# First layer's routing in three groups of batches instead of two, its first group placed ahead of the last batch; GpSimd stores the experts' results and SyncE only loads weights

## What is computed

```python
x = x + _L0_xattn_ref(_layernorm(x), ctx_768, ...)     # 16 heads of 16
x = x + _L0_ffn_ref(_layernorm(x), ...)
# _L0_ffn_ref, x of 800 rows by 256, 8 experts, hidden 1024:
gate_logits = jnp.einsum('btd,de->bte', x, Wg) + bg
gate_scores = jax.nn.softmax(gate_logits, axis=-1)
top1_idx = jnp.argmax(gate_scores, axis=-1)            # one expert for each row
h = jax.nn.silu(jnp.einsum('btd,edh->bteh', x, W1) + b1)
o = jnp.einsum('bteh,ehd->bted', h, W2) + b2
y = jnp.sum(o * top1_mask[..., None], axis=2) * top1_weight
...
x = x + _L1_xattn_ref(...)                              # second layer
x = x + _L1_ffn_ref(...)
```

## Time and profile before

| | |
|---|---|
| time, 3 runs | 704.38, 705.5, 707.92 us; median 705.5 |
| the profiled execution's own time | 702.82 us |
| its span, first to last instruction | 701.1 us |
| busy PE, PEld, DVE, ACT, POOL | 90%, 71%, 55%, 57%, 36% |
| mean granted clock of TensorE | 0.955 of full |
| first layer's routing and wait for rows | about 200 to 225 us |
| its experts | 225 to 314 us |

### The profile page before, as it was taken

One profiled execution on the slowest core, in us unless ns is written; L12 is line 12 of the kernel. 1 busy time (PEld: TensorE's weight loads), 2 busy tenths in 40 slices (PEclk: granted clock), 3 DMA queues, 4 the chain that ended last, 5 costly groups with the idle time before them and its releaser, 6 DMA issues.

```text
span 701.1 us, 15177 instructions
## 1 busy us (share of the span) xinstructions
PE 629.5 (90%) x4728; PEld 500.6 (71%) x4729; DVE 384.0 (55%) x1176; ACT 399.7 (57%) x961; POOL 249.3 (36%) x339
## 2 busy tenths in 40 slices
PE   2999789999986999989999989999997899999992
PEld 1777456666665888986788756666765798999992
DVE  5222467777734001108988754545775667666661
ACT  1444689998842334235576697767351455555550
POOL 6012355557647000002100000000032688888880
PEclk9999799999975999999999999999997999999995
DMA  6116910004431488403110010000022877677774
GB/s 153 32 47 203 328 48 2 2 1 152 134 115 40 147 274 279 148 33 91 35 49 8 0 52 1 1 2 1 1 94 71 222 194 189 179 188 195 191 186 119
DMA packets 76331, 73.76 MB, mean 105 GB/s; under 512 B 10966, under 2 KB 69876, under 8 KB 76152
## 3 DMA queue, kind: packets, MB, share of 16 engines
q1 hardware_dynamic: 69200, 64.45, 30.2%
q0 software_dynamic: 4240, 6.50, 5.1%
q10 hardware_dynamic: 2840, 2.17, 1.1%
HBM read 57.78 MB, written 15.31 MB: 104 GB/s over the span
## 4 chain that ended last, share of the span: by engine, by line
PE 60%; ACT 10%; DVE 9%; issue 7%; DMA 6%; POOL 4%; SPq 2%; DVEq 1%; POOLq 0%; ACTq 0%
PE psum L1254 4%; PE psum L1241 4%; ACT probs L793 4%; PE psum L630 3%; PE psum L644 3%; PE psum L1743 3%; PE psum L1765 3%; PE psum L1752 3%; DMA v_all<-in_L_ffn_W_dram 3%; PE psum L723 3%; PE psum L713 2%; PE psum L1791 2%; PE psum L2345 2%; PE psum L2347 2%; PE psum L2346 2%
## 5 line engine op out<-in xcount | busy, mean ns | idle before, releaser
L793 ACT ACTIVATE probs<-probs,negmax 100x361 f32<-100x361 f32 x128 | 68.9, 587 | 10.5 <-POOL probs L858 10.4
L873 DVE TENSOR_SCALAR_CACHE_REDUCE probs<-psum 100x361 f32<-100x361 f32 x128 | 60.6, 530 | 17.9 <-PE psum L713 17.9
L723 PEld LDWEIGHTS psum<-ident,probs 100*128 100x128 f32 (+1 forms) x384 | 39.4, 156 | 27.0 <-issue 18.7
L723 PE MATMUL psum<-ident,probs 100*128 100x100 f32 (+1 forms) x384 | 47.6, 262 | 11.1 <-ACT probsT L801 5.2
L858 POOL TENSOR_SCALAR probs<-probs 100x722 f32<-100x722 f32 x64 | 50.4, 788 | 5.1
L1284 ACT ACTIVATE kT_all<-psum,kT_all 128x128 f32<-128x128 f32 x88 | 25.1, 368 | 47.3 <-PE psum L1241 47.3
L2235 POOL TENSOR_TENSOR xT_low<-kT_all,xT_high 128x1600 fp32r<-128x1600 f32 x1 | 3.6, 3561 | 129.4 <-ACT xT_high L2206 129.4
L1241 PE MATMUL psum<-kT_all,v_all 128*128 128x128 f32 x352 | 43.4, 283 | 6.0 <-DMA v_all<-in_L_ffn_W_dram 2.9
L1241 PEld LDWEIGHTS psum<-kT_all,v_all 128*128 128x128 f32 x352 | 42.0, 198 | 8.9 <-issue 5.3
L2345 PE MATMUL psum<-xT_high,we_high 128*128 128x400 f32 x128 | 45.3, 354 | 2.9 <-issue 2.9
L2347 PE MATMUL psum<-xT_high,we_low 128*128 128x400 f32 x128 | 44.8, 350 | 0.0
(11 more groups left out here) (442 smaller groups left out, 1716.3 us busy)
## 6 DMA issues: line engine op xcount, KB each, us to landing
v_all<-in_L_ffn_W_dram SPq DMA_DIRECT2D x16, 1024.0 KB, 7.7
xs_dram<-zeros SPq DMA_DIRECT2D x1, 7424.0 KB, 23.5
kT_all<-coefT_dram SPq DMA_DIRECT2D x18, 400.0 KB
v_all<-in_L_ffn_Wg_dram SPq DMA_DIRECT2D x36, 128.0 KB
v_all<-in_L_ffn_Wu_dram SPq DMA_DIRECT2D x36, 128.0 KB
v_all<-in_L_ffn_Wd_dram SPq DMA_DIRECT2D x36, 128.0 KB
ctx_nat<-in_ctx_dram SPq DMA_DIRECT2D x16, 192.0 KB
rank_rows<-rank_dram SPq DMA_DIRECT2D x18, 100.0 KB, 3.5
```

What stands on the lines that cost most here:

```text
L723: last = nc.tensor.transpose(pT_ps[0:rows[t], t, hh * NQ:(hh + 1) * NQ], probs[:, n % NPB, hh, t * P:t * P + rows[t]], ident[0:NQ, 0:NQ])
L793: last = nc.scalar.activation(row, row, ACT.Exp, bias=negmax[:, n % NPB, hh:hh + 1])
L873: last = nc.vector.tensor_scalar(probs[:, n % NPB, hh, 0:NKV], psum[0:NQ, n % 2 * 2 + hh, 0:NKV], -CLAMP, None, ALU.max, ALU.max, accum_ou ...
```

## The change

It does eight things.

1. `sets` becomes three groups: batches 0 to 3, 4 to 6, and 7. The functions that had SET and two groups in them take each group's own size. Ranks of a later group start from `gate_prior_sums`, the sum of `choice` over all batches before, which DVE makes once a group (`gate_prior`), where a matmul for each batch did it before.
2. `begin_ranks`, `rank` and `gate_place` of group 0 move into the first attention, ahead of the last batch's transposes back and its addition.
3. The layer norm of batches 4 to 6 moves from POOL to DVE (`normalise0`); ACT loads the table of the square root with one extra instruction before it copies `take_tail`, and takes the roots after it.
4. `totals_ps` becomes one matmul over 64 columns in place of eight over 8; a reduction on DVE replaces the copy. The transposition of `b1` moves behind it.
5. On ACT the first block's rows are loaded before `act_top_weight`; DVE takes the sums after the first block's rows. PE's six products of zeros start when all groups are placed and the blocks are known, not after the second of three counts.
6. At the start of the first attention PE gets 12 products of zeros.
7. POOL stores `ys_rows` (`pool_experts`) and clears the spare rows of `sum_dram`; SP's loop over blocks goes.
8. SP loads W1 of expert e + 2 once the hidden layer of expert e's last block is done, and W2 once its output is; the signal `expert_begun` goes.

```diff
-    sets = [slice(k * SET, (k + 1) * SET) for k in range(2)]
+    sets = [slice(0, SET), slice(SET, B - 1), slice(B - 1, B)]
...
         for m in range(2):
             scores(m)
+            products_of_zeros0(o_zeros, 4 if m == 0 else 2)
         for m in range(M0):
             transposes(2 * m)
+            if m == 0:
+                products_of_zeros0(o_zeros, 2)
...
         finish_transpose(B - 1)
+        gate_transposes(pe, SET, B - 1 - SET)
+        begin_ranks(pe, 0)
+        rank(pe, 0)
         finish_transpose_back(B - 1)
-        gate_transposes(pe, SET, B - 1 - SET)
         finish_project(B - 1)
...
         finish_take(B - 1)
-        finish_takeT(B - 1)
         take_gate(act, 4, 2)
         take_gate(act, 6, 1)
+        finish_takeT(B - 1)
...
         dve_late_roots0(dve)
+        for k in range(SET, B - 1):
+            normalise0(k)
         gate_weigh(dve, 0)
+        gate_pick(dve, 0)
         normalise(B - 1)
-        gate_pick(dve, 0)
+        gate_prior(dve, 0)
+        gate_place(dve, 0)
         add(B - 1)
...
+    def gate_prior(dve, k):
+        dve.wait_ge(choice_ready, k + 1)
+        nc.vector.tensor_reduce(gate_prior_sums[k], choice[:, 0:sets[k].stop, :].rearrange("q b e -> q e b"), AX.X, ALU.add
+                                ).then_inc(prior_ready, 1)
...
         gate_weigh(dve, 1)
         gate_pick(dve, 1)
+        gate_prior(dve, 1)
         gate_place(dve, 1)
+        gate_weigh(dve, 2)
+        gate_pick(dve, 2)
+        gate_place(dve, 2)
...
-        step(dve, nc.vector.tensor_copy(tokens, totals_ps))
+        step(dve, nc.vector.tensor_reduce(tokens, totals_ps.rearrange("p (b e) -> p e b", b=B), AX.X, ALU.add))
...
+    def begin_ranks(pe, k):
+        nc.tensor.matmul(ranks_ps[k], ones_row[0:1, 0:NQ], region[:, 0:gate_shape(k)[1] * E0], start=True, stop=False)
+        if k > 0:
+            pe.wait_ge(prior_ready, k)
+            nc.tensor.matmul(ranks_ps[k], ones_sq[:, 0:NQ], gate_prior_sums[k - 1].unsqueeze(1).broadcast_to(gate_shape(k)),
+                             start=False, stop=False)
...
     def pe_gate(pe):
         gate_products(pe, SET, B - 1 - SET)
+        begin_ranks(pe, 1)
         gate_transposes(pe, B - 1, 1)
+        rank(pe, 1)
         gate_products(pe, B - 1, 1)
+        begin_ranks(pe, 2)
+        rank(pe, 2)
+        nc.tensor.matmul(totals_ps, ones_sq[:, :], choice[:, :, :], start=True, stop=True).then_inc(ranks_ready, 1)
...
+    def pool_experts(pool):
+        def block(n, at, i, p, first):
+            pool.wait_ge(ys_ready, n + 2)
+            pool.dma_start(ys_dram[bass.ds(at * P, P), :], ys_rows).then_inc(ys_stored, 16)
+
+        pool.dma_start(sum_dram[B * NQ:B * NQ + P, :], zeros[:, :]).then_inc(ys_stored, 16)
+        each_block(pool, block)
...
     def sp_experts(sp):
+        sp.wait_ge(slots_ready, 4)
+        for e in range(E0 - 2):
+            end = sp.value_load(per_expert_i[0:1, 2, e:e + 1], min_val=1, max_val=NBLK)
+            sp.wait_ge(hidden_in_psum, 2 * end)
+            sp_load_w1(sp, e + 2, e % 2)
+            sp.wait_ge(ys_in_psum, end)
+            sp_load_w2(sp, e + 2, e % 2)
...
-        pe.wait_ge(slots_ready, 2)
-        products_of_zeros0(6)
+        pe.wait_ge(slots_ready, 4)
+        products_of_zeros0(late_zeros, 6)
...
         load_rows(0)
+        act_top_weight(act)
         act.wait_ge(rows_used, 1)
...
         def _(pe):
             pe_project0(pe)
+            pe.wait_ge(consts_ready, N_CONSTS + N_MOE_CONSTS)
+            products_of_zeros0(o_zeros, 4)
```

140 lines of the change are left out of this document (62 added, 78 removed).

## The result

The changed kernel took 688.21, 689.04, 689.11 and 691.36 us, median 689.08; the kernel before, run beside it four times, had a median of 706.71 (704.38 to 709.43). The ratio is 0.9754, with an interval of 0.9709 to 0.9799: 2.5% faster. The profiled execution took 689.11 us with a span of 687.5, against 702.82 and 701.1, so 13.6 us of span are to be found. The medians lie 17.6 us apart: the profiled execution before was 3.9 us faster than the median of the four, while the one after stands at its median, and the profiles cannot say where those 4 us lie.

The account below looks back on a forecast made before the run. It saw time lost where PE stands or runs slowly, PE holding 60% of the last-ending chain. Terms -2.2 - 7.3 - 1.3 - 4.7 + 1.1 = -14.4 us gave 688.4 profiled, 691.1 as median; range 684 to 699.

Parts of the forecast that it names:

- Start of the attention: First attention: zeros on PE hold the clock for scores, transposes and values; -2.2 us, bounds +1.0 and -3.9.
- the bound of -3.9: Start of the attention: most the zeros could gain, from 7.9 us of half-speed PE work in a 10.4 us window.
- To the counts: Last batch and routing: norms on DVE, three groups and one totals matmul bring the counts 5.2 us earlier; bounds -3 and -6.
- To the load of rows: Counts to load of rows: fast cast, top weight out of the way, last scatter then late; -7.3 us in all, counts included.
- rival 1: Routing: POOL becomes the bound, load of rows gains 4 not 7.3 us, block 0 nothing of the clock; 695.7 us, chance 0.14.
- Block 0: First expert block: later zeros cut PE's idle time from 4.1 to 1.4 us, raising the clock; -1.3 us, bounds 0 and -1.7.
- Weights: Blocks 1 to 6: weights asked for two experts ahead, waits go and blocks last 7.26 us; -4.7 us, bounds -1.5 and -4.9.
- Rival 2: Experts: weights stay late because transfers set the pace at 268 GB/s; the term is -1.5, the time 694.3 us, chance 0.12.
- Rival 3: Start of the attention and block 0: the zeros do nothing at both places; 694.6 us, chance 0.10.
- Last store: End of the experts: DVE, SP and POOL wait for POOL's last store, which is not hidden; +1.1 us, between 0 and +1.3.
- Rival 4: Experts: POOL's stores hold DVE's bias addition, which waits for the previous block's store; slower, 712 us, chance 0.04.
- rival 5: Behind the experts: gain given back through gathers and keys starting late after POOL's loop; +10 us or more, 702 us, chance 0.05.

Follow-up runs that it names:

- e1: The changed kernel without its 12 products of zeros at the start of the first attention; median 703.34 us, ten runs from 688.43 to 710.29.
- e4: The changed kernel with the totals as eight matmuls of 8 columns and a copy, as before; 694.08 us in one run.
- e7: The changed kernel with one extra silu on ACT ahead of block 0, so its table loads early; median 690.38 us, ratio 0.9768 to the kernel before.
- e9: The kernel before with only the stores on POOL and SP loading weights two experts ahead, W1 and W2 apart; median 701.79 us, ratio 0.9932.
- after: The changed kernel itself, with all eight parts of the change, against the kernel before; median 689.08 us, ratio 0.9754.
- e2: The changed kernel with the top weight's work back ahead of the first load of rows on ACT and first rows on DVE; 694.01 us, one run.
- e3: The changed kernel with SP loading weights one expert ahead, asked for once PE begins an expert, stores still on POOL; median 691.56 us, ratio 0.9761.
- e8: The changed kernel with the early silu table, three zero products instead of four before first scores and five instead of six before block 0; median 691.16 us.
- e11: The changed kernel without the attention's startup zeros, but with 12 products of the same shape at the start of PE's program; median 688.51 us, ratio 0.9775.
- e12: The changed kernel, its zeros kept, with 12 more products at the start of PE's program; median 687.34 us, ratio 0.9765 to the kernel before.
- e6: The changed kernel without its six products of zeros ahead of block 0's rows; median 697.64 us, ratio 0.9913 to the kernel before.
- e10: The changed kernel with experts 0 and 1 written out ahead of PE's loop, so expert 0's block register loads before the transposes; median 691.54 us, ratio 0.9809.
- e5: The changed kernel with the experts' results stored from ACT's queue instead of POOL's; median 699.87 us, ratio 0.9907 to the kernel before.

## Why the prediction was right, and where not

**Start of the attention.** -2.2 predicted, -1.70 measured, by the mechanism named: no window near 0.5, scores at 0.87 us. From first scores to last values it is 2.0 us (120.9 to 118.9), less the 0.3 by which the first scores start later; `e1`, with the change's other edits in the attention but without the zeros, took 120.4, so up to 0.5 of the 2.0 may be theirs. The zeros were costed 0.3 us too short at each score (1.92 us for four). Taken away they cost 1.04 us in one kernel and 4.60 in another: the bound of -3.9 counted only the window up to 85 us, and the clock can stay low for longer.

**To the counts.** -5.2 predicted, 206.03 against 212.88 less the 1.70, so -5.15. Its parts: from the last values to the last batch's x -0.78 instead of -0.3, so -4.37 instead of -4.9 for the rest. The one product for the totals took 0.67 (0.5 taken), and `e4` gives 2.82 for it by itself. The projection was put at 1.0 us and took 1.39: the clock fell in the middle of it, and in other kernels with the same routing it took from 1.11 (`e1`) to 2.03 (`e7`). What is left beside the totals, the layer norms on DVE and the three groups, was read from rows only; no kernel undoes them one by one.

**To the load of rows.** -7.3 predicted, -7.40 measured. Cast at 0.16, load behind the last scatter, as forecast, and `e4` shows the scatter to be the bound by 1.4 us. The last scatter started at 207.91; from the predicted 209.3 less the start's 1.7, it was 0.3 us late. The Trainium skill's rule that GpSimd and VectorE share an interface, with contention for a VectorE instruction in a two-port mode or with two SBUF inputs ("GPSIMD Engine Reference", "1. Specifications"), agrees with the slow subtraction of both kernels in which they met, before and `e9` (2.28 us each), which has two inputs. The cast has one (1.65 and 2.27 us), and whether it ran in a two-port mode no trace shows. In after they miss each other by 0.08 us; the prediction had the subtraction behind the cast, near 211, but not that the moved transposition of `b1` gives it its place there, and put only 0.14 on rival 1.

**Block 0.** -1.3 predicted, -0.86 measured: the step mis-sized. The hidden layer fell to 3.83 as said, the zeros outlasted the rows by 0.7 us, but "block 0 should take 7.3" left out ACT's table load of 1.28 us. It had been hidden under the slow hidden layer before (226.57 in a layer that ended at 230.5) and was not hidden under the fast one. It lasted 8.20; `e7`, without the table load in the way, 7.39. The registers of PE's sequencer, part of the idle time ahead of block 0, were not seen either. That the clock held was in part luck: `e2` and `e3` have the same zeros, and `e8` five products for six, and their hidden layers took 5.46, 5.46 and 5.32 us.

**Weights.** -4.7 predicted, -4.11 measured; distances of 7.58 once, then 7.32 to 7.40, and not 7.26, but no wait for weights. `e3` separates what the prediction gave as three causes together: SP asked late because it stored first, and two experts ahead are not needed. Rival 2 is refuted: 273 GB/s were enough. Rival 3 is too, at the start by `e11` against `e12` (4.60 us); at block 0 `e6` shows the slow hidden layer, but its stop hides what the late zeros are worth in time.

**Last store.** +1.1 predicted, +0.72 measured. Issue to landing took 2.0 us, between the 1.7 of SP's store and the 3.0 of a gather; the latter was the wrong neighbour. The rest lies ahead of the issue, where POOL takes 0.68 us from DVE's addition. The Trainium skill's 0.4 us of difference in the first byte ("DMA: Bandwidth & Descriptors", "Specifications") is near the 0.3 measured from issue to landing, and the sum by it (+0.4) nearer in that part and too low in all. Rival 4, POOL's stores holding DVE, did not come: their median landing in the experts is 4.3 us after issue, and no DVE row there waits for a store.

**Behind the experts.** -0.23, nothing predicted, so rival 5 did not come; the same code varies by 5 us from kernel to kernel, so the 0.23 tells nothing. Sum: -14.4 predicted, -13.6 measured between the two profiled spans. As a median the prediction was 691.1, of which 2.7 us were the distance of the median before from its profiled execution; after had no such distance, so 689.08 lies below it although the span fell by less than forecast. That these two errors partly cancel is luck.

## What to carry to other kernels

When one link of a chain is shortened, work out which other one is late next and by how much: of the 2.82 us that the totals gave, half stayed under the scatters, and a table load that a slow clock had hidden came out when the clock rose. A queue that both asks for loads and waits for stores asks late; move the waiting one to an engine whose other work is not waited for (POOL here, not ACT). To test what filler products on TensorE are worth, move them instead of taking them out, since taking out can change more than the clock.

## What was not expected of the hardware

Both kernels with fewer instructions in PE's list than after by a whole group of products (`e1` and `e6`, twelve and six products) had stops of PE of 2.06 to 6.13 us in the first experts, after a weight load was issued, with no semaphore behind them; no kernel with as many or more had one (after, `e2`, `e3`, `e4`, `e7`, `e10`, `e11`, `e12`), nor had `e8` with two products less. The kernel before and `e9` had none either: they lack the twelve as well, but have seven products more in the totals and another order of ranks. In `e1` the stops were seen in one profiled execution. That PE then waited for its own instructions while the weights moved is my reading. The traces list instruction transfers too, in pieces of 16 KB (queue q8), and they support it: in each of the twelve kernels without a stop one such piece moved at the beginning of block 0, ahead of SP's first weight load of the stage (216.8 against 219.68 in after, 221.1 against 223.63 in `e11`, 227 against 237.50 before). In `e1` and `e6` none did; their next one came at 225.1 and 226.0, when weights were under way (loads at 224.24 and 224.97), and the first stops lie at 225.43 to 227.49 and 224.94 to 228.59. So the place in the list seems to matter because it sets when the next piece is fetched. It is not shown: the rows do not say for which engine a piece is, and the first stops end some 1.3 and 1.6 us after it has moved.

The gap ahead of block 0 decided its clock only in part: behind the late zeros, with 0.6 to 1.0 us of idle time it held (after, `e4`, `e5`, `e10`, `e12`), with 1.5 to 1.6 it held in `e1`, `e7` and `e11` and fell in `e2`, `e3` and `e8`.
